# Typed edge pass of a graph network: where GpSimd's gathers wait inside a block of 30

## What is computed

```
W = einsum('rb,bio->rio', comp, basis)
msg = node_feats[src] * norm
s = segment_sum(msg, etype * N + dst)
h = relu(einsum('rni,rio->no', s, W) + bias)
```

## Time and profile before

| | |
|---|---|
| median of three runs | 13042.21 us |
| time of the profiled execution | 13024.97 us |
| its span in the trace | 13023.2 us |
| POOL busy | 6424.3 us, 49% of the span |
| DVE busy | 6460.2 us, 50% |
| PE busy (matmuls) | 6886.8 us, 53% |
| ACT busy | 3557.6 us, 27% |

### The profile page before, as it was taken

How to read it: one execution, slowest core, us unless ns; L and a number is a source line. 1 busy time by engine, 2 the same in 40 slices (tenths; PEclk the granted TensorE clock), 3 DMA queues, 4 the chain that set the end, 5 groups by cost and what they waited for, 6 DMA issues and landing times. The chain is left out here.

```text
span 13023.2 us, 140147 instructions
## 1 busy us (share of the span) xinstructions
PE 6886.8 (53%) x48234; PEld 5140.2 (39%) x48282; DVE 6460.2 (50%) x6415; ACT 3557.6 (27%) x4717; POOL 6424.3 (49%) x6722
## 2 busy tenths in 40 slices
PE   9744444444444444444899999444444444444445
PEld 4322222222222222222899999333333323333334
DVE  4465665656556566565211211545545555455555
ACT  4344444444444444444100000211111111111112
POOL 4455555555555555553000000466666666666665
PEclk9866666666666666666999999666666666666667
DMA  9722222222222222222899898434334334343342
GB/s 389 305 84 80 80 89 80 79 90 80 79 89 80 80 84 85 80 80 93 320 391 365 336 393 347 114 93 96 95 93 98 93 94 98 93 96 95 93 98 65
DMA packets 462028, 1846.89 MB, mean 142 GB/s; under 512 B 174930, under 2 KB 241172, under 8 KB 349812
## 3 DMA queue, kind: packets, MB, share of 16 engines
q1 hardware_dynamic: 192948, 1168.03, 25.5%
q0 software_dynamic: 206272, 317.25, 10.9%
q10 hardware_dynamic: 62720, 360.50, 7.3%
HBM read 1270.37 MB, written 574.88 MB: 142 GB/s over the span
## 5 line engine op out<-in xcount | busy, mean ns | idle before, releaser
L1314 POOL DMA_INDIRECT big<-Pd,mt x3223 | 3048.6, 946 | 1706.0 <-issue 941.9
L552 PE MATMUL ps<-ring 128*128 128x490 bf16 x3223 | 1486.9, 554 | 3130.9 <-DVE ring L479 1486.2
L476 DVE TENSOR_TENSOR ring<-ps,vw 128x2940 bf16<-128x2940 f32 x538 | 1730.9, 3217 | 2223.4 <-remote 1641.1
L442 POOL DMA_INDIRECT big<-Yd,ix x1620 | 1532.4, 946 | 1265.8 <-issue 692.6
L442 POOL DMA_INDIRECT gv<-Yd,ix x1603 | 1516.2, 946 | 1234.8 <-issue 700.7
L552 PEld LDWEIGHTS ps<-ring 128*128 128x128 bf16 x3223 | 421.3, 131 | 3983.2 <-issue 2031.0
L587 ACT ACTIVATE Z<-ps 128x490 f32 x1620 | 1157.8, 715 | 1656.4 <-remote 850.2
L1343 DVE TENSOR_TENSOR ps<-ps,big 128x1024 f32<-128x1024 f32 x403 | 481.9, 1226 | 2237.8 <-DMA big<-Pd,mt 2222.7
L587 ACT ACTIVATE big<-ps 128x490 f32 x1603 | 1152.8, 719 | 1605.1 <-remote 840.7
L1407 ACT ACTIVATE big<-ps 128x1024 bf16<-128x1024 f32 x269 | 275.5, 1024 | 3539.4 <-issue 3519.4
L1450 PE MATMUL ps<-idt,total 128*128 128x128 f32 x135 | 64.0, 474 | 1883.2 <-issue 1668.1
(11 more groups left out here) (217 smaller groups left out, 11779.1 us busy)
## 6 DMA issues: line engine op xcount, KB each, us to landing
Yd<-big SPq DMA_DIRECT2D x196, 1024.0 KB, 8.8
Aj<-Z SPq DMA_DIRECT2D x54, 3136.0 KB
Aj<-big SPq DMA_DIRECT2D x54, 3136.0 KB
big<-Aj SPq DMA_DIRECT2D x108, 1568.0 KB, 8.5
cb<-Aj ACTq DMA_DIRECT2D x108, 1568.0 KB, 9.4
cb<-Aj SPq DMA_DIRECT2D x108, 1568.0 KB, 8.9
Z<-Aj ACTq DMA_DIRECT2D x108, 1568.0 KB, 8.7
dr<-in_dstr SPq DMA_DIRECT2D x135, 1152.0 KB
```

Of the source, the lines that this page charges most:

```text
L442: e.indirect_dma_start(gv[j][:, k, 0:64], None, table, bass.IndirectOffsetOnAxis(ap=ix[j][:, k:k + 1], axis=0)).then_inc(sm[f"g{j}"], 16)
L476: nc.vector.tensor_tensor(one[r][:, 0:m, :], bc_t(iof, m, W * NT), bc_f(vw[j][:, k], m, W * NT), ALU.is_equal)
L552: nc.tensor.matmul(PS[q][:, 0:W * NT], olo[r][:, c, :], one[r][:, c, :], start=True, stop=False)
L1314: e.indirect_dma_start(gv[j][:, k, :], None, Pd, bass.IndirectOffsetOnAxis(ap=mt[j][:, k:k + 1], axis=0)).then_inc(sm[f"g{j}"], 16)
```

## The change

The wait at the 24th gather goes. Two others come in. The 16th gather (k = 15) of block b waits for `cm1` to reach 5·b-2, which is triple 5 (the sixth) of turn b-1, the one beside it. The 26th gather (k = 25) waits for `pe` to reach b+1, which is the sum by nodes of turn b-1, block b-1 being the one ahead. The block's next wait (`pe` at b+1 before block b+1's first gather) is the same count, so it is met already when POOL comes to it. The last five gathers of a block and the first 15 of the next are thus one run with no wait on PE in it, and gathers 16 to 25 are another.

```diff
-                    done = reg(e, TH * b)
+                    third, summed = reg(e, TH * b - 2), reg(e, b + 1)
                     for k in range(LA if last else KA):
-                        if k == 23 and not first:
-                            e.wait_ge(sm["cm0"], done)
+                        if k == 15 and not first:
+                            e.wait_ge(sm["cm1"], third)
+                            e.sem_inc(sm["pool"], 1)
+                        if k == 25 and not first:
+                            e.wait_ge(sm["pe"], summed)
                             e.sem_inc(sm["pool"], 1)
```

## The result

The changed kernel takes 12614.61 us (median of four runs, 12601.85 to 12633.83); the kernel before, measured beside it, 13045.79 us. The ratio is 0.967, with an interval of 0.9653 to 0.9686. The forecast was 12,780 us within 12,400 to 13,250: right in its sign and its range, while the gain is 431 us instead of 262. The runs that follow add a condition to it: in some submissions the kernel before doesn't lose these microseconds at all, and kernels that differ from the changed one by a single wait bring nothing there. One of the seven executions of the kernel before beside e7_three fell in a slower state (14325 us at a granted clock of 0.582), and the interval of that ratio leaves it out.

A forecast was written before the change was run, and what follows sets the result against it. Bound: PE's messages stuck while POOL gathers, losing 13 us of each 51.5 us turn. A turn of 46.8 + 1.5 + 0.7 = 49.0 saves 262 us over 105 turns, giving 12,780 us, range 12,400 to 13,250.

The forecast's parts named there:

- Where the loss lies: Typed pass: 13 us of each 51.5 us turn are lost to something that POOL's gathers bring with them.
- The release: PE's stuck messages come free when POOL pauses, the last 1.8 to 9.0 us after its stop, 0.15 us per gather.
- Caught again: Rival, chance 0.22: triple 6's message stays stuck until POOL's second stop; turn 58.3 us, time 13,756 us.
- The first run: POOL's twenty gathers from the sum on take 25.1 us and stop at 25.8 of the turn, instead of 29.5.
- The pause: At POOL's new wait, triple 5's message is free at 28.0 and the second run begins at 28.6.
- Triple 6 and group 4: Last held message comes 3.7 us after POOL's stop; DVE's group 4 starts at 29.5 instead of 33.7, 4.2 us earlier.
- The first deduction: Triple 6's message may be held longer because POOL already gathers again: nothing to 4.2 us, taken as 1.5.
- From group 4 to the next turn: Rest of the turn, with the sum, takes 17.3 us beside gathers (15.3 without); the turn ends at 46.8.
- The failed pause: Triple 5's message comes before POOL stops, so POOL runs 30 gathers: 0.06 of turns, 12 us longer, 0.7 on average.
- The sum: Total for the typed pass: a turn of 49.0 instead of 51.5 us, 262 us less over 105 turns.
- The point of sticking moves forward: Rival, chance 0.10: triple 4 is stuck too and group 3 starts at 28.0; turn 52.0 us, time 13,095 us.
- The gathers aren't the cause: Rival, chance 0.08: where POOL pauses doesn't matter; the turn stays at 51.5 us, the time at 13,042 us.

The follow-up runs named there:

- e7_three: Changed kernel with waits at the 11th gather (triple 4) and 21st (triple 8) instead of the 16th and 26th; 12846.0 us, 0.983 of the kernel before.
- e1_k15: Changed kernel without its wait at the 26th gather, in a submission that holds no messages; 10870.4 us, 1.000 of the kernel before.
- e6_k15: Changed kernel without its wait at the 26th gather, in a submission that holds messages; 12757.2 us, 0.979 of the kernel before.
- e10_k13: Changed kernel with its first wait at the 14th gather on triple 6, instead of the 16th on triple 5; 12546.5 us, 0.969 of the kernel before.
- e8_k25: Changed kernel without its wait at the 16th gather, so POOL gathers in runs of 30; 13701.6 us, 1.048 of the kernel before.
- e11_busy: Changed kernel with its wait at the 16th gather replaced by subtraction work on POOL; 12515.9 us, 0.966 of the kernel before.

## Why the prediction came out right, step by step

*Where the loss lies.* Right, in the submissions that have it. The last turn, with only 13 gathers beside it, that stood for what is possible (38 us) is what e1_k15 does all the time, 37.4 us.

*The release.* Right for the last held message, and now shown over a wider range. From POOL's last gather to the last held message it took 3.0 us after 15 gathers (e6_k15), 3.4 after 18 (e10_k13), 3.7 after 20 (2980.24 - 2976.56), 5.1 after 30 (e8_k25). The line 0.7 + 0.147 per gather gives 2.9, 3.3, 3.6 and 5.1. "The stuck ones come free when POOL pauses" is too wide, though. Earlier messages can come free inside a run, and the trace of before had it already. The turn that begins in the earlier trace rows at 4158.83 goes on:

```profile
4185.60 2.29 ACT L587 ACTIVATE big<-ps 128x490 f32 x3 [4.08 <-issue]
...
4191.80 0.94 POOL L442 DMA_INDIRECT big<-Yd,ix  x1 [0.30 <-issue]
```

Triple 5 had ended at 4180.3 and triple 6 at 4185.4. ACT sees triple 5 at 4185.60, 7.1 us before POOL's stop; triple 6 is seen only at 4196.64, 3.9 us after it. In 38 of the loop's 104 turns triple 5's message comes like this, with POOL in its run and triple 6 done and unseen. The prediction says that no turn of before has such a message (under "Caught again"); that is a misreading. It did no harm, because group 4 waits for triple 6, and triple 6's message came behind the stop in all 104.

*The first run.* Stop forecast at 25.8, measured 25.7.

*The pause.* Triple 5's message was forecast at 28.0 and POOL's restart at 28.6. In 80 turns they came at 29.4 and 30.0, and both held messages came together at the end of the release. In 20 turns they came at 28.7 and 29.3, apart from triple 6, as the forecast had it.

*Triple 6 and group 4.* Forecast 29.5, measured 29.3 in the 80 turns and 30.0 in the 20. **The first deduction is the term that was mis-sized.** It took 1.5 us for a message that might be held again because POOL starts before it. In the 80 turns it measured nothing: triple 6's message is there (2980.24) before POOL starts (2980.92). In the 20 POOL starts first (3123.72), and the message comes 0.7 us later (3124.45) and not at the second stop. The mean is 0.1. So "caught again" had its chance in 20 turns and did not happen.

*From group 4 to the next turn.* Forecast 17.3, measured 18.6 in the turn shown (2998.82 - 2980.24) and 18.1 on average in the 80. Before, ACT could copy triple 5 2 us before group 4 began; now both start together, and PE's triple 7 waits for ACT's copy (the row at 2982.89). The 20 other turns bear this out: ACT copies triple 5 1.3 us before group 4 begins, the way to the next turn takes 16.7, and the turn is 0.8 shorter though group 4 starts 0.7 later. Once the messages are free, it is ACT's copy of triple 5 as much as group 4 that everything hangs on. That was not in the sum.

*The failed pause.* Forecast 6% of the turns at 12 us, 0.7 on average. Measured five of 105 at some 8 us, 0.4. They were cheaper because in three of them triple 6's message came free before POOL's stop.

*The sum.* 46.8 + 1.5 + 0.7 = 49.0 was forecast. Measured: an ordinary turn of 47.3 and 0.4 for the long ones, 47.7. The difference of 1.3 us over 105 turns is 137 of the 165 us between forecast and result. Another 20 are the distance of the profiled execution from the median: the forecast added 17 for it, and now it lay 4 above (12,618). The parts were off by 0.5 one way (the way from group 4 was longer) and 1.8 the other (the two deductions were too large); that they cancel in part is luck.

*The rivals.* "The point of sticking moves forward" did not come out (group 3 waited 0 to 6 us for triple 4, not 12). "The gathers aren't the cause" is refuted in submissions like the one of the forecast by e8_k25, e11_busy and the rests of e7_three. The rule of the Trainium skill behind it (SBUF — State Buffer, section Who interferes with whom: PE and ACT never wait on anyone) stands in a section on the ports of SBUF, so it was a wide reading to apply it to semaphores. So read, it agrees with the submissions that take 10,870 us and not with the others, where PE's own rows in the sum halt beside POOL's gathers and go on when they rest.

*Still open.* What on PE sets the point at which it sticks. It is not the time since POOL began alone: that was some 15 us for triples 4 and 5, but the run of seven in the earlier trace rows, which ends at 4161.76 and so began at 4153.3, held triple 0, which PE had done within a microsecond of 4158.83, some 6 us into the run and with most of the sum in it. A count of matmuls and weight loads since POOL last rested for more than 1 us can be fitted to these places, but that is argued and not shown. Triple 5 is held after 57 rows of both kinds and triple 9 of e7_three after 54. PE itself halts after 115 in e6_k15, 109 in e10_k13 and 110 in e7_three, and triple 0 of the earlier trace rows has 113. The run that was to decide came in a submission that holds nothing. Why some held messages come free inside a run is open too, and so is what makes a submission hold at all. One trait of the traces goes with it: the nine traces in which messages are held have 45,788 to 59,974 recorded semaphore updates for the whole kernel, the five others 142,575 to 142,927. Whether the updates are missing from the record only, or are themselves what sticks, no run tells.

## What to carry to other kernels

Where engines wait for "remote" beside a long row of indirect gathers, look at how late the last message is after the gathers' next rest: here 0.7 us + 0.15 per gather of the run. Then place the rests where a message is due, as long as that release takes, and let no long run of gathers lie beside a long row of matmuls on PE. A rest need not be a wait. And look through all turns before one is taken for the rule: the two kinds of ordinary turn and the messages that come free inside a run show only then.

Run the same kernel in more than one submission before such tuning. Here it is worth 3% in some, and its like nothing in others, while the loss it works around is 17%.

## What the runs showed of the hardware

The same program takes 12,960 to 13,070 us in some submissions and 10,870 in others, with a gather of 944 to 946 ns in both. Where it is slow, PE's semaphore counts come late while GpSimd issues indirect gathers (triple 5's by 12 us in the median turn of the kernel before and of the changed one, by 16 in e8_k25), and in a longer run PE's own instructions halt; single rows of fp32 matmuls then come about 2 us apart (e6_k15). The last held count comes 3.0 us after 15 gathers, 3.7 after 20, 5.1 after 30. A rest of 1.0 us frees nothing, one of 2.7 us after ten gathers (e7_three) and one of 3.7 after 15 (e6_k15) everything that was held, and other work on GpSimd (4.39 us of it) does nearly as well as idleness.
